# A transformer tower with routed experts: embedding sums, variances and one-hots from VectorE to GpSimd, four engines in a new order, and the last stage's output ahead of its norm

## What is computed

```python
x = emb[tokens] * sqrt(D) + positional_encoding
scores = einsum('d,bijd->bij', attn_scale, tanh(q[:, :, None, :] + k[:, None, :, :]))
x = layer_norm(x + softmax(scores) @ v @ Wo, g1, beta1)
x = layer_norm(x + relu(x @ W1 + bf1) @ W2 + bf2, g2, beta2)          # token layer
h = x + attention8(layernorm(x))                                      # second attention
n = ln(h, ln1);  vals, idx = top_k(softmax(n @ Wr @ codebook.T / T), 2)
moe = sum over the two experts of w * (silu(n @ W1[e] + b1[e]) @ W2[e] + b2[e])
hmoe = moe + 0.25 * (silu(n @ Ws1 + bs1) @ Ws2 + bs2)
out = h + hmoe + silu(ln(hmoe, ffln) @ Wf1 + bf1) @ Wf2 + bf2
```

## Time and profile before

| | us |
|---|---|
| median of three runs | 800.54 (799.36 to 802.94) |
| profiled execution | 801.53 |
| its span | 799.5 |

### The profile page before, as it was taken

The page is one execution under the profiler, slowest core; times in us unless marked ns, Lnnn a source line. Parts: engine busy times, 40 slices in busy tenths (PEclk is TensorE's granted clock), DMA queues, the critical chain, the costliest instruction groups (busy, mean ns, idle before and its releaser), DMA issues.

```text
span 799.5 us, 21390 instructions
## 1 busy us (share of the span) xinstructions
PE 743.0 (93%) x7238; PEld 594.1 (74%) x7238; DVE 611.6 (76%) x1634; ACT 615.2 (77%) x1455; POOL 366.5 (46%) x482
## 2 busy tenths in 40 slices
PE   2767999999999999999999999986899899999898
PEld 1454776776777777777777777765799899998787
DVE  4999899999999999999999996533434345433785
ACT  2787899999999999999999998763356465655454
POOL 3211234456465465465465455766047355554121
PEclk9999899999999999999999999997999999999999
DMA  2950000000000000000000000001599999993501
GB/s 79 251 120 6 5 5 7 12 17 14 12 16 14 12 16 17 12 16 17 12 17 16 12 12 12 17 20 31 175 384 375 402 395 365 346 359 119 168 29 39
DMA packets 50096, 78.99 MB, mean 99 GB/s; under 512 B 7428, under 2 KB 34203, under 8 KB 50000
## 3 DMA queue, kind: packets, MB, share of 16 engines
q1 hardware_dynamic: 33824, 65.01, 23.8%
q0 software_dynamic: 5664, 7.92, 3.7%
q10 hardware_dynamic: 10512, 4.83, 2.2%
HBM read 63.95 MB, written 15.92 MB: 100 GB/s over the span
## 4 chain that ended last, share of the span: by engine, by line
PE 75%; DVE 6%; issue 4%; SPq 4%; DMA 3%; ACT 2%; POOL 2%; POOLq 0%; DVEq 0%; ACTq 0%
PE b_s L1385 15%; PE b_o L1539 7%; PE big L1695 6%; PE big L1498 6%; PE big L1505 5%; PE big L1519 5%; DVE arena L941 4%; PE b_y L1482 3%; PE b_qk L1706 3%; PE b_s L1706 3%; PE big L1526 3%; PE big L1751 3%; DMA arena<-in_wpack 3%; PE big L1470 3%; PE b_s L1764 2%
## 5 line engine op out<-in xcount | busy, mean ns | idle before, releaser
L941 DVE TENSOR_TENSOR arena<-qT,b_qk 128x2304 f32<-128x2304 f32 x128 | 323.9, 2536 | 0.1
L688 ACT ACTIVATE arena<-arena 128x2304 f32<-128x2304 f32 x128 | 275.6, 2156 | 17.6 <-DVE arena L941 17.6
L1385 PE MATMUL b_s<-arena,apad 128*32 128x192 f32 x3072 | 155.7, 339 | 9.1 <-ACT arena L688 9.0
L1385 PEld LDWEIGHTS b_s<-arena,apad 128*32 128x32 f32 x3072 | 89.4, 112 | 78.6 <-issue 29.1
L849 ACT ACTIVATE act_h<-big,arena 128x128 f32<-128x128 f32 x324 | 92.4, 368 | 71.5 <-PE big L1695 71.5
L656 POOL DMA_INDIRECT eo_dram<-gT,toff x81 | 79.7, 984 | 95.0 <-DVE gT L1270 91.3
L1695 PE MATMUL big<-hbT,arena 128*128 128x128 f32 x648 | 87.0, 278 | 5.3 <-DMA arena<-in_wpack 3.9
L578 POOL TENSOR_TENSOR kept<-kept,rs 96x384 f32<-96x384 f32 x64 | 52.8, 824 | 78.1 <-DVE rs L1077 77.7
L750 ACT ACTIVATE kept<-big,mx 96x96 f32<-96x96 f32 x256 | 83.6, 354 | 1.7 <-DVE mx L1071 1.5
L1695 PEld LDWEIGHTS big<-hbT,arena 128*128 128x128 f32 x648 | 79.6, 193 | 6.2 <-issue 5.5
L1259 DVE TENSOR_SCALAR hbT<-b_t,cols 128x128 f32<-128x128 f32 x81 | 33.2, 409 | 61.5 <-PE b_t L1688 61.5
(11 more groups left out here) (226 smaller groups left out, 1441.8 us busy)
## 6 DMA issues: line engine op xcount, KB each, us to landing
arena<-in_wpack SPq DMA_DIRECT2D x81, 578.0 KB, 9.1
prT<-rows_dram ACTq DMA_DIRECT2D x73, 64.5 KB
rows_dram<-act_h SPq DMA_DIRECT2D x1, 4128.0 KB, 24.1
arena<-eo_dram SPq DMA_DIRECT2D x4, 512.0 KB, 7.1
x_dram<-res SPq DMA_DIRECT2D x16, 96.0 KB, 1.7
out<-of SPq DMA_DIRECT2D x12, 128.0 KB, 1.8
eo_dram<-gT,toff POOLq DMA_INDIRECT x81, 5.6
rows_dram<-rows_now,slots POOLq DMA_INDIRECT x64, 2.3
```

The lines of the kernel that those rows point to most:

```text
L688: act.activation(v, v, ACT.Tanh).then_inc(s["tanh"], 1)
L941: dve.tensor_tensor(ring[c % TRING].rearrange("p (x m n) -> p x m n", m=CQ, n=N), qv.unsqueeze(3).to_broadcast([D, SPLIT * QG, CQ, N]), kv ...
L1385: last = pe.matmul(b_s[32 * a:32 * a + 32, 0:SPLIT * N], apad[:, 31 - line:63 - line], t[:, :, a, m, :], start=(line == 0), stop=(line == ...
```

## The change

In the tower, `x_rows` goes from DVE (one instruction: multiply and add) to POOL (a multiply, a wait for it, an add). The variances of the four norms go into POOL's `root` and `roots_h1`, ahead of the power and with a wait between; `means` on DVE signals `var_...` itself. `one_hot` goes from DVE (one instruction over four expert numbers) to POOL (four instructions, each with its expert number as a scalar per token). DVE's first `queries` waits for the constants. All four bodies have a new order, and with it the three tables; of these, two lines stand here.

In the last stage `rh` is made by POOL's new `last_residual`, which waits for `mixed` and stands ahead of the root. `hm` has two buffers and `rh` four. `mixture` ends with the variance, the norm is a function `f_rows`, and DVE runs `mixture(j)`, `output(j - 2)`, `f_rows(j)`, where it ran the norm ahead of the output.

```diff
-RESIDUALS = 3
+RESIDUALS = 4
...
-    (4, "pr_turn 0"), (5, "shared 1"), (4, "scores 2"), (4, "scores 3"), (4, "pr_turn 1"), (4, "heads_m 0"),
...
+    (4, "pr_turn 0"), (4, "scores 2"), (5, "shared 1"), (4, "heads_m 0"), (4, "pr_turn 1"), (4, "scores 3"),
...
-        hm = sb("hm", [128, G, D])
+        hm = [sb(f"hm_{i}", [128, G, D]) for i in range(2)]
...
+        rh.append(gT_cols[:, 10 * D:12 * D].rearrange("p (g d) -> p g d", g=G))
...
+            def x_rows(p):
+                wait(pool, s["xs_t"], p)
+                if p < EARLY:
+                    pool.wait_ge(s[f"emb{p}"], 16 * G)
+                else:
+                    pool.wait_ge(s["emb2"], 16 * G * (p - (EARLY - 1)))
+                if p == 0:
+                    pool.wait_ge(s["ld_a"], 16 * 5)
+                wait(pool, s["kept"], p)
+                pool.tensor_scalar(xs[:, :, :], pair_of(res, p) if p < EARLY else emb[:, :, :],
+                                   float(np.float32(D) ** np.float32(0.5)), None, ALU.mult).then_inc(s["scaled"], 1)
+                pool.wait_ge(s["scaled"], p + 1)
+                pool.tensor_tensor(xs[:, :, :], xs[:, :, :], pe_rows[:, :].unsqueeze(1).to_broadcast([N, G, D]),
+                                   ALU.add).then_inc(s["xs"], 1)
+
...
             def root(p, n):
                 pool.wait_ge(s["var_" + n], p + 1)
+                pool.tensor_scalar(ve[n][:, :], mv[n][:, :, 1], EPS if n == "h0" else EPS_TOK, None, ALU.add)\
+                    .then_inc(s["ve_" + n], 1)
+                pool.wait_ge(s["ve_" + n], p + 1)
                 pool.tensor_tensor(rstd[n][:, :], ve[n][:, :], halves[:, 0:G], ALU.pow)\
                     .then_inc(s["rstd_" + n], 1)
 
             def roots_h1(p):
+                wait(pool, s["shift"], p)
                 pool.wait_ge(s["var_h1"], p + 1)
+                pool.tensor_scalar(ve_h[:, 0:G], mv["h1"][:, :, 1], EPS, None, ALU.add)
+                pool.tensor_scalar(ve_h[:, G:3 * G].rearrange("p (a g) -> p a g", g=G),
+                                   mv["h1"][:, :, 1].unsqueeze(1).to_broadcast([N, 2, G]),
+                                   1.0 + EPS, EPS * EPS, ALU.mult, ALU.add).then_inc(s["ve_h1"], 1)
+                pool.wait_ge(s["ve_h1"], p + 1)
                 pool.tensor_tensor(rstd_h[:, :], ve_h[:, :], halves[:, :], ALU.pow).then_inc(s["rstd_h1"], 1)
 
...
+            def one_hot(p):
+                wait(pool, s["slot"], p)
+                pool.wait_ge(s["topf"], p + 1)
+                for g in range(G):
+                    for k in range(TOPK):
+                        j = g * TOPK + k
+                        last = pool.tensor_scalar(oh[:, g, k, :], iota_e[0:N, :], of_pair(topf, p)[:, j:j + 1], None,
+                                                  ALU.is_equal)
+                last.then_inc(s["hot"], 1)
 
...
+            def last_residual(j):
+                pool.wait_ge(s["mixed"], j + 1)
+                if j >= RESIDUALS:
+                    pool.wait_ge(s["of"], j - RESIDUALS + 1)
+                pool.tensor_tensor(rh[j % RESIDUALS], hm[j % 2][:, :, :],
+                                   xr[:, j, :].rearrange("p (g d) -> p g d", g=G), ALU.add).then_inc(s["rh"], 1)
+
             def rstd_last(j):
                 pool.wait_ge(s["fve"], j + 1)
                 pool.tensor_tensor(frstd[:, :], fve[:, :], fhalf[:, :], ALU.pow).then_inc(s["frstd"], 1)
 
             for j in range(NB):
+                last_residual(j)
                 rstd_last(j)
 
 
...
-            def x_rows(p):
-                wait(dve, s["xs_t"], p)
-                wait(dve, s["kept"], p)
-                if p < EARLY:
-                    dve.wait_ge(s[f"emb{p}"], 16 * G)
-                else:
-                    dve.wait_ge(s["emb2"], 16 * G * (p - (EARLY - 1)))
-                dve.scalar_tensor_tensor(xs[:, :, :], pair_of(res, p) if p < EARLY else emb[:, :, :],
-                                         float(np.float32(D) ** np.float32(0.5)),
-                                         pe_rows[:, :].unsqueeze(1).to_broadcast([N, G, D]),
-                                         ALU.mult, ALU.add).then_inc(s["xs"], 1)
-
...
-            def variance(p, n):
-                ch.wait_for("mv_" + n)
-                if n == "h1":
-                    wait(dve, s["tn"], p)
-                if n != "h1":
-                    dve.tensor_scalar(ve[n][:, :], mv[n][:, :, 1], EPS if n == "h0" else EPS_TOK, None,
-                                      ALU.add).then_inc(s["var_" + n], 1)
-                else:
-                    dve.tensor_scalar(ve_h[:, 0:G], mv[n][:, :, 1], EPS, None, ALU.add)
-                    dve.tensor_scalar(ve_h[:, G:3 * G].rearrange("p (a g) -> p a g", g=G),
-                                      mv[n][:, :, 1].unsqueeze(1).to_broadcast([N, 2, G]),
-                                      1.0 + EPS, EPS * EPS, ALU.mult, ALU.add)\
-                        .then_inc(s["var_h1"], 1)
+                last.then_inc(s["var_" + n], 1)
...
-            def one_hot(p):
-                ch.wait_for("topf")
-                dve.tensor_tensor(
-                    oh[:, :, :, :].rearrange("p g k e -> p (g k) e"),
-                    iota_e[0:N, :].unsqueeze(1).to_broadcast([N, G * TOPK, E]),
-                    of_pair(topf, p).unsqueeze(2).to_broadcast([N, G * TOPK, E]), ALU.is_equal)\
-                    .then_inc(s["hot"], 1)
...
             def mixture(j):
                 dve.wait_ge(s[f"er{result_sem(j)}"], 16)
-                for k, (src, dst) in enumerate([(ysh[:, j, :].rearrange("p (g d) -> p g d", g=G), hm1), (hm1, hm)]):
+                mixed = hm[j % 2]
+                if j >= 2:
+                    dve.wait_ge(s["rh"], j - 1)
+                for k, (src, dst) in enumerate([(ysh[:, j, :].rearrange("p (g d) -> p g d", g=G), hm1), (hm1, mixed)]):
                     for g in range(G):
                         last = dve.scalar_tensor_tensor(dst[:, g, :], er[:, j, TOPK * g + k, :],
                                                         wts[:, G * j + g, k:k + 1], src[:, g, :], ALU.mult, ALU.add)
-                    ch.link(last)
-                    ch.wait()
-                for g in range(G):
-                    last = dve.bn_stats(fstat[:, g, :], hm[:, g, :])
+                    if k == 0:
+                        ch.link(last)
+                        ch.wait()
+                    else:
+                        last.then_inc(s["mixed"], 1)
+                        dve.wait_ge(s["mixed"], j + 1)
+                for g in range(G):
...
                 ch.wait()
                 dve.tensor_scalar(fve[:, :], fmv[:, :, 1], EPS, None, ALU.add).then_inc(s["fve"], 1)
-                ch.link(dve.tensor_tensor(rh[j % RESIDUALS], hm[:, :, :], xr[:, j, :].rearrange("p (g d) -> p g d", g=G),
-                                          ALU.add))
+
+            def f_rows(j):
+                dve.wait_ge(s["frstd"], j + 1)
+                if j:
+                    dve.wait_ge(s["fT_ps"], j)
+                for g in range(G):
+                    last = dve.tensor_scalar(fn[:, g, :], hm[j % 2][:, g, :], fmv[:, g, 0:1], frstd[:, g:g + 1],
+                                             ALU.subtract, ALU.mult)
+                last.then_inc(s["fn"], 1)
+
+            def output(j):
+                dve.wait_ge(s["rh"], j + 1)
+                dve.wait_ge(s["f2"], j + 1)
+                if j:
+                    dve.wait_ge(s["out"], 16 * j)
+                for g in range(G):
+                    last = dve.tensor_tensor(of[:, g, :], [b_s, b_qk][g][:, 0:D], rh[j % RESIDUALS][:, g, :], ALU.add)
+                last.then_inc(s["of"], 1)
+
+            for j in range(NB):
+                mixture(j)
                 if j == 0:
                     for i in range(NB - 2, NB):
                         shared_rows(i)
-                dve.wait_ge(s["frstd"], j + 1)
-                if j:
-                    dve.wait_ge(s["fT_ps"], j)
-                for g in range(G):
-                    last = dve.tensor_scalar(fn[:, g, :], hm[:, g, :], fmv[:, g, 0:1], frstd[:, g:g + 1],
-                                             ALU.subtract, ALU.mult)
-                last.then_inc(s["fn"], 1)
-
-            def output(j):
-                dve.wait_ge(s["f2"], j + 1)
-                if j:
-                    dve.wait_ge(s["out"], 16 * j)
-                for g in range(G):
-                    last = dve.tensor_tensor(of[:, g, :], [b_s, b_qk][g][:, 0:D], rh[j % RESIDUALS][:, g, :], ALU.add)
-                last.then_inc(s["of"], 1)
-
-            for j in range(NB):
-                mixture(j)
                 if j >= 2:
                     output(j - 2)
-            ch.wait()
+                f_rows(j)
             output(NB - 2)
             output(NB - 1)
 
```

(56 more changed lines are left out.)

178 lines of the change are left out of this document (89 added, 89 removed), and 6 rows, old and new, of the table BIG_ORDER.

## The result

The changed kernel takes 808.98 us (median of four runs) where the kernel before takes 801.74: ratio 1.0091, 95% interval 1.0065 to 1.0117. It is slower by 0.9%, the forecast was 798.4, and the range ended at 807.

What follows compares the result with a forecast made beforehand. The tower's period was taken as mainly PE's order, the last stage's as DVE waiting for POOL's root. +3.9 - 1.9 - 2.6 + 1.3 - 2.8 = -2.1 gave 798.4 us for the median, range 790.5 to 807.

Steps and rivals of the forecast that it cites:

- Start: Kernel start: x_rows(0) on POOL stands behind iotas and a large memset, so everything behind moves by +3.9 us.
- Fill: Up to some 86 us: DVE sets the pace and loses x_rows, variances and one x1_norm, -1.9 us, other end 0.
- Steady tower: Thirteen pairs: relief of DVE brings back 0.2 us a pair, -2.6 us, from 0 to -9.6.
- The pause of 0.57 and 0.55: Before each of eight scores a pair: taken as PE's price for changing to the 32-column matmul, in us.
- POOL too late: Steady tower: POOL's last normalisation, behind two scatters and two gathers, makes PE wait 0.8 us a pair; 808.8 us, chance 23%.
- DVE was the bound: Steady tower: DVE sets the period, so a pair falls by 0.74 us until ACT is full; 791.4 us, chance 22%.
- Drain: Last pair: one-hots and variances in series on POOL ahead of the counts, +1.3 us, between +0.6 and +3.5.
- Last stage: Residual sum on POOL, output in DVE's wait: PE becomes the bound at 3.73 us a block, -2.8 us, bounds -1.0 and -2.8.

Runs made afterwards that it cites:

- the ACT swap: Changed kernel with ACT's copy of the fourth quarter of gT ahead of the first softmax's exponential: ratio 1.0083 to the kernel before.
- the gathers: Changed kernel with POOL's two embedding gathers behind the first norm's root: 805.39 us; with ACT's copy ahead of the exponential too, 803.31 us.
- the two misses: Changed kernel with the last pair's fourth quarter in its old place, 811.05 us; changed kernel with the last four pairs' variances and one-hots on DVE, 805.10 us.

## Why the prediction was wrong

- *Start* (+3.9): right; 3.88, the multiply 0.88 where 0.89 was taken. That it carries to the end is shown.
- *Fill* (-1.9): -3.1 measured to the fifth pair; to the fourth pair's queries and keys at 86.53, where the forecast ended the fill, it is -2.25. DVE's relief alone does not bring it: the moved instructions in the old orders bring 0.5, the orders alone 0.8, both together 3.1 (steps of the first four pairs). What joins them was not tried.
- *Steady tower* (-2.6, bounds 0 and -9.6): the first step that failed; +2.9 over eleven pairs. Two things in it were wrong. The 0.2 us a pair that DVE's relief was to bring are nothing in the old order: with the relief alone the step is 30.57. And the upper bound of 0 took PE's new order to be no worse than the old one. It is better in itself (30.3 to 30.5 where nothing holds it) but it depends on ACT's copy and on POOL's normalisation at places that leave no room. The order was in view, with its rows, and I priced only the instructions that left DVE. The pause of 0.57 and 0.55 before the scores' weight loads was not a fixed price of PE's either: in the steady tower of the changed kernel none is over 0.4, while the score matmuls take 8.90 us a pair as before.
- *POOL too late* (the rival with 23%): right in its place and its cause, shown by the ACT swap and the gathers. In the changed kernel itself its sign did not show (a step above 30.9 and a wait for `kept`), because the wait for ACT's copy came first. Its size was not right: I counted 0.8 us a pair against the forecast's step of 30.35, and it is 0.45, shared with the chain through ACT. That its 808.8 lies next to the measured 809.0 is a coincidence of terms, since drain and fill differ too.
- *DVE was the bound* (22%): refuted for the kernel before; with the moved instructions alone DVE's busy time fell by 1.3 in 50 and the step did not move. The rule of the Trainium skill, "Perfetto Trace Analysis", section Identifying the Most-Contended Engine, would have named DVE here by its occupancy of 99.6%; the run contradicts that use of it, and PE's list of waits, empty, was the better sign.
- *Drain* (+1.3, bounds 0.6 and 3.5): +6.3, the second step that failed, by 5.0 us where the tower's missed by 5.5; the prediction's last sentence, that nothing but the tower weighs 4 us, was wrong. One-hots were mis-sized: 438 ns for 64 columns, as much as line 584's 445 for 128, where I took 300 by the number of columns. In the old orders they and the variances cost 3.05, within the bounds: 1.7 behind the logits, where the one-hots lie (0.9 taken), and 1.3 ahead of them (0.4 taken, with three norms in series where a pair passes four). The orders' 3.0 have no term in the sum at all.
- *Where the orders' 3.0 lie.* Counted from the last pair's queries and keys, in three traces:

| us after queries and keys | before | new orders alone | after |
|---|---|---|---|
| maximum of the first softmax | 36.99 | 37.01 | 36.30 |
| its turned result enters the value product | 41.83 | 45.01 | 44.22 |
| second norm | 61.86 | 65.12 | 65.44 |
| logits | 93.83 | 96.52 | 98.28 |

With the new orders alone the lateness is there at the value product, 3.2 us, before anything that the fourth quarter's place or POOL's later work could change. That agrees with the two misses. PE's timeline has it between two instructions, the turn of the softmax and that product, before and with the new orders alone:

```profile
492.71 0.38 PE L1447 MATMUL b_t<-ident,p 128*96 128x128 f32 x2
...
495.13 0.69 PE L1455 MATMUL b_y<-vrow,p1T 96*96 96x130 f32 x4
```

```profile
500.83 0.38 PE L1447 MATMUL b_t<-ident,p 128*96 128x128 f32 x2
...
506.11 0.69 PE L1455 MATMUL b_y<-vrow,p1T 96*96 96x130 f32 x4
```

2.4 us became 5.3, and PE has no wait in them: it runs the older pairs' products, which the new order puts between the two. The same distance grows in every pair (from the maximum to the value product some 5.9 us before, 9.8 to 10.0 in the steady tower of the new orders), and only the last pair pays for it in full. That the lateness arises here is seen; a run with these two instructions moved back together was not made. Whether a part of it is only a matter of where one counts (a shorter fill beside a longer drain) is not shown; fill, by the steps of the first four pairs, and drain together are 211.9 before and 215.2 after.
- *Last stage* (-2.8): right in size and in mechanism, also by itself; the sum took 0.72, as the Trainium skill's rule on ports ("SBUF — State Buffer", Who interferes with whom) had it beside statistics with one input.

## What to carry to other kernels

When an engine is full and another one, also full, has no wait in its list, take a few per cent from the first alone and look at the step before believing in it: here 1 us less on VectorE moved nothing in the old order, and 0.7 us a step in the new one. A new hand-written order has to be priced by its tightest hand-overs, each with its slack in us, not by the work it moves; two chains with 0.1 us between them hid each other here, so a repair that moves only the name in the list of waits is half of one. Work that is hidden in the steady loop was paid in full where the loop starts and ends, and so was a longer distance between two stages of one pair; such work can be left on the old engine for the first and the last turn.

## What was not expected of the hardware

GpSimd's comparison of 64 columns with a scalar per partition took 438 ns, the multiply-add of 128 columns (line 584) 445, and the multiply of 256 columns by a constant 862, more than the sum of two inputs of that shape (724). The first has half the columns of the second and takes as long; they differ in operation too, so no rule for the columns is drawn. An addition to two columns (the variance) took 0.22 us, three times the 0.07 that it cost VectorE's stream.
